# One V buffer instead of two in a cross-attention kernel, with new hand-written engine orders

## The reference

```python
Q = (q @ Wq + bq).reshape(b, s, H, DH).transpose(0, 2, 1, 3)     # b 16, s 512, H 16, DH 64
K = (k @ Wk + bk).reshape(b, s, H, DH).transpose(0, 2, 1, 3)     # k and v are the context
V = (v @ Wv + bv).reshape(b, s, H, DH).transpose(0, 2, 1, 3)
scores = jnp.einsum('bhqd,bhkd->bhqk', Q, K) / jnp.sqrt(jnp.float32(DH))
scores = scores * mask
attn = jax.nn.softmax(scores, axis=-1)
ctx = jnp.einsum('bhqk,bhkd->bhqd', attn, V)
ctx = ctx.transpose(0, 2, 1, 3).reshape(b, s, H * DH)
out = ctx @ Wo + bo
x = q + out
mu = jnp.mean(x, axis=-1, keepdims=True)
var = jnp.var(x, axis=-1, keepdims=True)
return (x - mu) * jax.lax.rsqrt(var + LN_EPS) * gamma + beta
```

## Time and profile before

| | us |
|---|---|
| time, median of 3 runs | 2202.15 (2201.57 to 2203.34) |
| the profiled execution: its own time | 2204.18 |
| its span, first to last instruction | 2202.4 |
| PE busy | 2099.0 (95%) |
| DVE busy | 1947.7 (88%) |
| ACT busy | 1787.5 (81%) |
| POOL busy | 1030.6 (47%) |
| granted TensorE clock, mean | 0.984 |

### The profile page before, as it was taken

The page is one execution under the profiler, slowest core; times in us unless marked ns, Lnnn a source line. Parts: engine busy times, 40 slices in busy tenths (PEclk is TensorE's granted clock), DMA queues, the critical chain, the costliest instruction groups (busy, mean ns, idle before and its releaser), DMA issues.

```text
span 2202.4 us, 37555 instructions
## 1 busy us (share of the span) xinstructions
PE 2099.0 (95%) x12348; PEld 883.9 (40%) x12348; DVE 1947.7 (88%) x4283; ACT 1787.5 (81%) x3809; POOL 1030.6 (47%) x1576
## 2 busy tenths in 40 slices
PE   2689999999999999999999999999999999999985
PEld 1234444444444444444444444444444444444432
DVE  6779899999989999998999999899999989999882
ACT  3669798797978879797887969889797988979791
POOL 2116264362735437273553737355372635537244
PEclk9799999999999999999999999999999999999997
DMA  6368879797897978799797979979797897979683
GB/s 224 72 120 167 179 139 212 134 192 155 176 201 128 215 136 187 158 168 206 131 208 142 184 160 175 201 136 198 147 186 158 168 211 132 196 144 184 136 162 87
DMA packets 1117603, 364.00 MB, mean 165 GB/s; under 512 B 1073504, under 2 KB 1073504, under 8 KB 1117408
## 3 DMA queue, kind: packets, MB, share of 16 engines
q1 hardware_dynamic: 1114288, 361.58, 82.0%
q10 hardware_dynamic: 3120, 0.01, 0.1%
HBM read 76.30 MB, written 16.78 MB: 42 GB/s over the span
## 4 chain that ended last, share of the span: by engine, by line
PE 91%; DVE 4%; DMA 2%; POOL 1%; ACT 1%; issue 1%; POOLq 0%; ACTq 0%; DVEq 0%; SPq 0%
PE fill_ps L390 21%; PE fill_ps L391 19%; PE fill_ps L392 19%; PE score_ps L443 16%; PE ctx_ps L464 15%; DVE score_ps L917 1%; DMA pT<-p 1%; DVE p L931 1%; DMA bv_col<-in_L_xattn_bv 1%; DVE small L799 1%; PE ctx_ps L377 0%; ACT probs L615 0%; DVE wk L836 0%; DVE wq L836 0%; POOL acc L1261 0%
## 5 line engine op out<-in xcount | busy, mean ns | idle before, releaser
L615 ACT ACTIVATE probs<-score_ps,neg_max 128x512 f32<-128x512 f32 x1024 | 692.2, 687 | 154.4 <-POOL neg_max L1216 146.0
L917 DVE CUSTOM_DVE_ANT_0 score_ps<-score_ps,mask_sb,small 128x512 f32<-128x512 f32 x1024 | 724.0, 754 | 100.1 <-PE score_ps L443 97.1
L629 ACT ACTIVATE p<-probs,inv_sum 128x512 f16<-128x512 f32 x1024 | 674.3, 720 | 100.6 <-DVE inv_sum L925 89.6
L931 DVE SCALAR_TENSOR_TENSOR p<-probs,inv_sum,p 128x512 f16<-128x512 f32 x896 | 697.9, 816 | 12.0 <-ACT p L629 10.2
L1216 POOL TENSOR_SCALAR neg_max<-row_max 128x2 f32<-128x2 f32 x512 | 155.3, 303 | 689.8 <-DVE row_max L917 689.7
L443 PE MATMUL score_ps<-k,q 64*128 64x512 f16 x3072 | 388.4, 379 | 11.3 <-ACT probs L615 5.7
L464 PE MATMUL ctx_ps<-pT,v 128*64 128x512 f16 x3072 | 359.8, 384 | 18.5 <-DMA pT<-p 14.5
L464 PEld LDWEIGHTS ctx_ps<-pT,v 128*64 128x64 f16 x3072 | 165.6, 110 | 205.2 <-issue 76.5
L1222 POOL TENSOR_SCALAR down_sum<-row_sum 128x4 f32<-128x4 f32 x256 | 76.2, 298 | 357.2 <-ACT probs L615 349.2
L443 PEld LDWEIGHTS score_ps<-k,q 64*128 64x128 f16 x3072 | 127.5, 94 | 251.5 <-issue 99.3
L615 ACT ACTIVATION_READ_ACCUMULATOR probs<-score_ps,neg_max 128x1 f32 x1024 | 210.4, 205 | 0.0
(11 more groups left out here) (91 smaller groups left out, 2960.4 us busy)
## 6 DMA issues: line engine op xcount, KB each, us to landing
raw<-in_xt SPq DMA_DIRECT2D x64, 256.0 KB, 3.4
raw<-in_ct SPq DMA_DIRECT2D x64, 256.0 KB, 3.5
mask_sb<-in_mask_Bx1xSxS_fk SPq DMA_DIRECT2D x64, 256.0 KB, 3.6
acc<-in_x SPq DMA_DIRECT2D x64, 256.0 KB, 3.7
out<-acc SPq DMA_DIRECT2D x64, 256.0 KB, 2.8
pT<-p SPq DMA_TRANSPOSE x512, 4.6
wq_staged<-in_L_xattn_Wq SPq DMA_DIRECT2D x4, 512.0 KB, 7.3
wk_staged<-in_L_xattn_Wk SPq DMA_DIRECT2D x4, 512.0 KB, 11.2
```

The lines of the kernel that those rows point to most:

```text
L615: nc.scalar.activation(probs[:, i % E_TILES, :], score_ps[:, i % 4, :], ACT.Exp, bias=neg_max[:, p % 2, i:i + 1], accum_out=row_sum[:, p % ...
L629: nc.scalar.activation(p16[:, q, a, 0, :], probs[:, i % E_TILES, :], ACT.Copy, scale=inv_sum[:, p % 2, i:i + 1]).then_inc(p_rounded, 1)
L917: nc.vector.tensor_tensor_reduce(out=score_ps[:, i % 4, :], in0=score_ps[:, i % 4, :], in1=mask_sb[:, q, :], scale=score_scale, scalar=-3. ...
L931: nc.vector.scalar_tensor_tensor(out=p16[:, q, a, 1, :], in0=probs[:, i % E_TILES, :], scalar=inv_sum[:, p % 2, i:i + 1], in1=p16[:, q, a, ...
```

## The change

- `v16` has one half: `v16[:, g % 1]`. V blocks 4 to 7 overwrite blocks 0 to 3 of the same batch, so the round of block 4 waits for the values of pair 3 of this batch, and the round of the next batch's block 0 for those of pair 7 of this batch.
- `values` of pairs 0 and 4 wait for all four V blocks at once, ahead of their matmuls.
- `ones` is a 128x128 array and not a 128x1 column read with a broadcast.
- `FILL_BANK`, and every engine's `body`, are written anew. The set of calls in a body is the same on every engine; only their order differs. V4 to V7 now stand between v3 and v4, V0 and V1 of the next batch just ahead of v7, V2 after it.

```diff
-        v16 = sb("v16", [P, 2, KT, 2, GW], F16)
+        v16 = sb("v16", [P, 1, KT, 2, GW], F16)
...
-        ones = sb("ones", [P, 1])
+        ones = sb("ones", [P, P])
...
                 for q in range(QT):
                     pe.wait_ge(pT_in[par][q], turn_no(n, p))
+                if p % GROUP == 0:
+                    pe.wait_ge(v_split, n * 2 * KT + (g + 1) * KT)
...
                 for t in range(KT):
-                    if p % GROUP == 0:
-                        pe.wait_ge(v_split, n * 2 * KT + g * KT + t + 1)
...
-                            mm = nc.tensor.matmul(ctx_ps[a * DH:(a + 1) * DH, :], v16[:, g, t, piece, col:col + DH],
+                            mm = nc.tensor.matmul(ctx_ps[a * DH:(a + 1) * DH, :], v16[:, g % 1, t, piece, col:col + DH],
...
-                    if k % KT == 0 and not is_first(n):
-                        act.wait_ge(pv_ready, (n - 1) * PAIRS + (k // KT + 1) * GROUP)
-                    nc.scalar.activation(v16[:, k // KT, k % KT, 0, :], bank, ACT.Copy, scale=v_scale).then_inc(
+                    if k % KT == 0 and not (is_first(n) and k < 1 * KT):
+                        act.wait_ge(pv_ready, n * PAIRS + k // KT * GROUP)
+                    nc.scalar.activation(v16[:, k // KT % 1, k % KT, 0, :], bank, ACT.Copy, scale=v_scale).then_inc(
```

More of the change, by code:

```diff
@@ L294, in body @@
                     start()
+                if here is not None:
+                    transpose_probs(here, 0, range(2, 4))
+                if nxt is not None:
+                    load_input(nxt, "x", range(0, 1))
                 if prev is not None:
@@ L307, in body @@
[L307 to L310, removed]
+                    transpose_probs(here, 1, range(0, 1))
+                if prev is not None:
+                    load_acc(prev, range(2, 4))
+                if here is not None:
+                    transpose_probs(here, 1, range(1, 3))
+                if nxt is not None:
+                    load_input(nxt, "c", range(1, 3))
@@ L477, in body @@
                     users.update((FILL_BANK[f"{kind}{k}"], fill_read(here - 1 + ahead, kind, k))
-                                 for kind, k, ahead in (("V", 2, 1), ("K", 2, 1), ("O", 0, 0)))
+                                 for kind, k, ahead in (("V", 0, 1), ("O", 0, 0), ("V", 2, 1)))
                 if here is not None:
                     fill(here, "K", 3)
+                    fill(here, "Q", 3)
+                    scores(here, 2, range(2, 4))
                     fill(here, "V", 3)
-                    fill(here, "Q", 3)
-                    fill(here, "V", 4)
-                    scores(here, 2, range(2, 4))
-                    values(here, 0)
                     fill(here, "K", 4)
-                    scores(here, 3, range(0, 2))
                 if prev is not None:
@@ L523, in body @@
                 if here is not None:
-                    scores(here, 7, range(0, 1))
                     values(here, 4)
-                    scores(here, 7, range(1, 2))
                 if nxt is not None:
@@ L529, in body @@
                 if here is not None:
-                    values(here, 5)
                     scores(here, 7, range(2, 4))
@@ L533, in body @@
                     fill(nxt, "K", 0)
+                    fill(nxt, "K", 1)
+                if here is not None:
+                    values(here, 5)
+                if nxt is not None:
+                    scores(nxt, 0, range(0, 2))
                 if opening:
@@ L728, in body @@
                 if here is not None:
-                    exponentials(here, 6, range(4, 6))
+                    round_probs(here, 6, range(1, 2))
                 if nxt is not None:
@@ L750, in body @@
                 if here is not None:
-                    round_probs(here, 7, range(0, 3))
+                    round_probs(here, 7, range(1, 2))
+                    exponentials(here, 7, range(4, 5))
+                    round_probs(here, 7, range(2, 3))
                 if nxt is not None:
@@ L754, in body @@
                 if here is not None:
-                    exponentials(here, 7, range(4, 6))
+                    exponentials(here, 7, range(5, 8))
                     round_context(here, 5)
-                    exponentials(here, 7, range(6, 8))
+                    round_probs(here, 7, range(3, 8))
+                if nxt is not None:
+                    exponentials(nxt, 0, range(0, 1))
                 if opening:
@@ L1269, in body @@
             def body(prev, here, nxt, first):
+                if here is not None:
+                    scale_sums(here, 2, 0)
                 if prev is not None:
@@ L1327, in body @@
                     scale_input(nxt, "x", range(2, 3))
+                if here is not None:
+                    scale_sums(here, 6, 0)
+                    negate_max(here, 6, range(2, 3))
+                if nxt is not None:
                     split_input(nxt, "x", range(2, 3))
```

593 lines of the change are left out of this document (294 added, 299 removed).

## The result

| | before | after |
|---|---|---|
| time, median of 4 runs on the same chip, us | 2201.89 | 2216.32 (2215.03 to 2217.55) |
| ratio, 95% interval | | 1.0063, 1.0048 to 1.0079 |
| the profiled execution: own time, span | 2204.18, 2202.4 | 2216.15, 2214.4 |

What follows compares the result with a forecast made beforehand. PE was taken to bound the usual batch, with no waits. The terms +1.7 +0.2 +0.7 -2.2 -4.7 sum to -4.3 us on the span of 2202.4, giving a forecast of 2198 beside 2202.15, range 2190 to 2212.

Steps and rivals of the forecast that it cites:

- Steady batches: Usual batches: one more change of matmul kind, +1.7 us over 15 batches, plus 0.2 us in all for new stalls.
- The walk: PE's new list set out on its own clock, with ACT and DVE walked along it at 0.65 and 0.67 us an instruction.
- V blocks 4 to 7: Between v3 and v4 in a batch: the single V buffer's new wait on pair 3 costs nothing.
- The tight point: V7 uses V4's bank, so needs V4 split: at about 76.2, wanted at 76.6, slack 0.4 us.
- The rival of a stall in every batch: V7 waits for V4's split, or S51 for an exponential: at 0.8 us a batch, 2210; chance 0.27.
- The opening: Before K3: context and maxima of v later, what follows shorter, maxima of o near 98.5; +0.7 us, bounds -1.5 and +4.
- The first batch: From K3 to v1: 7.8 us lost instead of 10.2, v1 starting at 146.3; term -2.2 us, bounds -4 and 0.
- The end: Last batch: tile 7 split 5.3 us sooner, 3.4 to 5.9 reaching v7; term -4.7 us, bounds -1.5 and -6.
- the rival in which the transposes hold the end: Last batch: transposes queue, DMA being 86% busy in a batch, and the 4.7 us gain is gone: 2202.5; chance 0.12.
- The clock in the opening: PE may be at 1.2 GHz, not 2.4, when the context comes, since x arrives in pieces from 33 to 43 us.
- the rule weighed: TensorE's clock is throttled unless recently active; by it Q1, K0 and K1 run slowly, costing 5 to 7.5 us.
- a rival at +5 us: Opening: 24 matmuls of K0 and K1 at the lower clock, +5 us instead of +0.7: 2202; chance 0.08.

Runs made afterwards that it cites:

- run 5: Changed kernel with POOL writing zeros by memset instead of subtracting for the low halves of x and context: 2197.94 us, 0.9979 of the kernel before.
- run 7: Changed kernel with DVE's splits of tiles 1 to 4 of pair 6 touching only 8 of 512 columns: 2209.04 us, ratio 1.0028.
- run 8: Changed kernel with POOL writing zeros for the low halves of x and context in four memsets of 128 columns each: 2199.27 us, ratio 0.9983.
- run 4: Changed kernel's orders with two V halves again, ACT's waits as before and `ones` one column: 2216.82 us, ratio 1.0061.
- run 10: Kernel before with only POOL's order in the last full batch changed, `scale_out`, `shift_out` and `add_bo` behind tile 7: 2202.66 us, ratio 0.9994.
- run 11: As run 10, plus in the last full batch PE's S72 and S73 ahead of v5 and ACT's two `standardize` behind pair 7's rounds: 2202.74 us, ratio 0.9996.
- run 12: As run 10, plus ACT's two `standardize` behind pair 7's rounds in the last full batch, PE's order left: 2201.32 us, ratio 0.9995.
- run 1: Changed kernel with POOL's `scale_biases` behind `negate_max(6, 1)` instead of ahead of it: 2218.43 us, ratio 1.0071.
- run 2: Changed kernel with DVE splitting the next batch's Q1 ahead of tiles 1 and 2 of pair 7's probabilities: 2212.92 us, ratio 1.0045.
- run 3: Changed kernel with `scale_biases` behind `negate_max(6, 1)` and the next batch's Q1 split ahead of pair 7's tiles 1 and 2: 2210.69 us, ratio 1.0035.
- run 9: Run 3 plus order edits: opening's `scale_biases` behind context tile 2, first batch's Q4 split earlier, last full batch's `scale_out` behind tile 7: 2207.20 us, ratio 1.0019.

## Why the prediction was wrong, point by point

**Steady batches: the step that failed.** It is "I put 0.2 us in all for the new stalls", with the durations under it, "0.67 us for each mask or split on DVE". Measured: 1.00 us more a batch, 14.0 over the fourteen from bound to bound, of which new waits are 1.03 us a batch (0.17 of old ones went, and the one more change of kind adds its 0.11). The walk priced a split at its length alone, but a split costs 0.66 to 1.7 us depending on what POOL does beside it, and the new lists put the splits of pairs 6 and 7 beside POOL's reading of the context. Runs 5, 7 and 8 show it in three ways. For the usual batch the prediction walked ACT's and DVE's queues and never POOL's, whose share of 47% gave no reason to; the wait of S63 stood in that queue. The row that could have warned me was there: DVE's mean for a split was 816 ns in the profile of before, well over 0.67. Both signs of being wrong that the prediction had named came: a batch over 129.9 us, and a last transpose that POOL's tile 7 did not release.

**V blocks 4 to 7.** Right in the usual batch: V7 waited for nothing, v4 neither, and run 4 shows that a second buffer gives nothing back in the time. The tight point that I named, V4's split, held. Only in the last batch, where the fill of the next Q0 that I called the cover is missing, does v4 wait 0.36 us for V7's split, and v0 of the first batch waits 0.50 for a V block; run 4 has both, so they come with the orders and the one wait for four blocks.

**The rival of a stall in every batch** had the right side and about the right size (0.8 us a batch and 2210 for the measured 1.00 and 2216), and a wrong mechanism. The stalls are not of the single buffer by itself. Whether they follow from it by a longer way (V4 to V7 late, so the context's buffer is free late, so POOL's work on the context is pushed beside the splits of pair 6) is argued from the lists and not shown. From the end of V7's fill to nK0 the new list leaves 11.0 us where the old one had 14.6 (steps and changes counted in the two lists). The small waits of S50 to S53 stay in runs 5 and 8 too; their cause stays open.

**The opening**, +0.7: right in size, as far as it can be told. The maxima of v start at 55.13 (I said 57), those of o at 98.70 (98.5), K3 at 114.50 (before 114.29). Other executions of the same openings start K3 at up to 115.33 (before, runs 10 to 12) and 115.95 (after, runs 1 to 4 and 7), a mean difference of 0.3 us, so 98.70 beside 98.5 is partly luck. Run 9 shows that POOL's place of `scale_biases`, which the walk let vanish behind DVE, costs there.

**The first batch**, -2.2: measured about 0. From K3 to v1 it is 34.6 us instead of 37.0, but the new list has 24.4 us of work there where the old one had 26.8, so 10.2 are lost as before. My sign for it ("v1 some 2.4 us sooner in relation to K3") came true as it was worded and shows nothing of the term. PE there, against the earlier trace rows:

```profile
141.48 0.61 PE L436 MATMUL score_ps<-k,q 64*128 64x512 f16 x1 [4.57 <-DVE q L948]
142.26 2.79 PE L436 MATMUL score_ps<-k,q 64*128 64x512 f16 x11 [0.18 <-ACT probs L608]
144.99 0.61 PE L383 MATMUL fill_ps<-cT,wk 128*128 128x512 f16 x1
```

The window there (its granted clock is the last number but two):

```profile
142.00:146.00 4.00, 3.82 (x15) 1.09 (x15) 4.00 (x10) 2.59 (x8) 0.42 (x1) 0.50 0.91 167
```

PE stood still for 4.57 us and came back at 1.2 GHz (0.50). From 142.26 S40 and S41 took 2.73 us instead of 1.4 and K5 4.10 instead of 2.7, 2.7 us in all; v1 started at 149.1, right behind K5, where the walk had 146.3. The split context that the walk had it wait for was done at 145.26. The term left out the clock's price after a wait.

**The end**, -4.7: -3.7, counted from the last batch's K3 to the end of the span (2065.38 to 2214.4, before 2049.74 to 2202.4). Of that v7's start is 2.9 us nearer, where I had said 4 to 5; most of the rest is that v7 took 4.40 us instead of 5.33, at a better clock, which I had not forecast. Right in kind. I had written that the last transpose would be released by POOL's tile 7. That was done at 2165.96; the last transpose but one waited for DVE's splits until 2166.5 and the last went right behind it, at 2167.07. The splits were stretched to 5.38 us beside POOL's `scale_out`, in DVE's timeline:

```profile
2161.13 5.38 DVE L933 SCALAR_TENSOR_TENSOR p<-probs,inv_sum,p 128x512 f16<-128x512 f32 x4
```

and in POOL's:

```profile
2160.36 2.94 POOL L1276 TENSOR_TENSOR acc<-acc,gamma_b 128x512 f32<-128x512 f32 x2
```

Run 9 took that away, and the queue of transposes and the clock took its place. So the rival in which the transposes hold the end did not come in the changed kernel (PE's two waits for them sum to 11.8 us in its page, 14.5 before), but its queue stands in runs 9 to 12, where the splits ahead are done sooner, and leaves v7 at most 1.1 us of what tile 7 and the splits gained.

**The clock in the opening** (the rule weighed, and a rival at +5 us): half of Q1's fill still ran 0.43 us a matmul, the lower level's spacing, until 45.5 us. From there on, K0 and K1 included, it was 0.216. PE had caught up by 49.44, where K0 waited 0.48 us for POOL's context, so the slow part cost nothing and the rival did not come.

## What to carry to other kernels

When an order is moved by hand, walk every engine's queue, and price an instruction by what runs beside it: here a VectorE instruction with two SBUF inputs cost up to 2.3 times its length beside a GpSimd instruction that reads. A mean duration above the shortest one of the same shape is the sign of it. A wait that an edit removes may only move: removing S63's wait gained nothing, both edits of order brought back half of the loss, and the rest went only when the splits ran at their length. And read a sum by its stretches: run 9 hit its total with both terms wrong.

## What the runs showed of the hardware that I had not expected

The stretching goes both ways and does not depend on the amount of data: two GpSimd instructions on 8 columns went from 0.35 (alone, in run 5) to 1.34 us beside VectorE's splits of 512 columns, which kept their 0.67. Such an instruction can be held for more than one split: in run 3 it begins at 959.37, beside the second of four splits in a row (958.57 to 961.30), and ends at 961.37, after the last. A GpSimd write of zeros beside the same kind of splits kept its length (0.64 us for four) while the read after it took 1.78 instead of 0.70. And in the opening of after the fill matmuls from 38 to 45.5 us stand 0.43 us apart while the granted clock of the windows 38 to 42 and 42 to 46 us reads 1.00, so that there the spacing is the better witness of the speed.
